# Relation layer of a two-layer graph network: squares on ScalarE and the rows' factor in PSUM, in place of two VectorE operations whose operands both lie in SBUF

## The reference, cut to what matters

```
h_tan   = log_map_zero(h)                                  # per node
msg_tan = einsum('ei,eio->eo', h_tan[src], rel_weight[etype]) + rel_emb[etype]
msg     = tanh(sc*|msg_tan|) * msg_tan / (sc*|msg_tan|)     # sc = 0.1
w       = en / (norm_sum[dst] + 1e-6)
lam     = 2 / (1 - 0.01*sum(msg*msg) + 1e-6)
numer   = segment_sum(w*lam * msg, dst);  denom = segment_sum(w*lam, dst)
h_agg   = project_to_ball(numer / denom)                    # then combined with the loop term
```

## Time and profile before

| | us |
|---|---|
| median of 3 runs | 6124.92 |
| the profiled execution's own time | 6125.32 |
| its span, first to last instruction | 6123.5 |
| POOL busy | 4091.2 |
| VectorE busy | 3449.4 |
| TensorE matmul busy | 2752.4 |
| ScalarE busy | 1127.1 |

### The profile page before, as it was taken

How to read it: one execution, slowest core, us unless ns; L and a number is a source line. 1 busy time by engine, 2 the same in 40 slices (tenths; PEclk the granted TensorE clock), 3 DMA queues, 4 the chain that set the end, 5 groups by cost and what they waited for, 6 DMA issues and landing times.

```text
span 6123.5 us, 55029 instructions
## 1 busy us (share of the span) xinstructions
PE 2752.4 (45%) x13577; PEld 1954.7 (32%) x13578; DVE 3449.4 (56%) x3558; ACT 1127.1 (18%) x1409; POOL 4091.2 (67%) x3714
## 2 busy tenths in 40 slices
PE   2540000000000000000677788788878787877777
PEld 1110000000000000000555566555656565655555
DVE  8601121212122222231688888888888888888887
ACT  3540000000000000000222222222222222222322
POOL 2327777777777777756466666667666666677663
PEclk6555555555555555555788888888888888888888
DMA  5881111111111111101000010001001010101110
GB/s 148 276 252 31 23 28 34 26 36 38 24 39 39 27 35 39 31 5 22 21 21 15 19 29 21 21 21 28 22 21 29 21 29 21 29 21 29 29 29 19
DMA packets 150773, 252.22 MB, mean 41 GB/s; under 512 B 73462, under 2 KB 130315, under 8 KB 135158
## 3 DMA queue, kind: packets, MB, share of 16 engines
q0 software_dynamic: 126224, 100.13, 8.4%
q1 hardware_dynamic: 24431, 151.31, 7.2%
q10 hardware_dynamic: 32, 0.01, 0.0%
HBM read 113.60 MB, written 136.63 MB: 41 GB/s over the span
## 4 chain that ended last, share of the span: by engine, by line
POOL 28%; PE 20%; DVEq 15%; issue 15%; DVE 13%; DMA 6%; POOLq 1%; ACT 1%; SPq 0%; ACTq 0%
POOL arena L354 25%; PE psS L573 9%; DVEq L1226 7%; PE psS L578 6%; DVE stage L1187 4%; DMA table<-arena 4%; PE psW L567 3%; DVE stage L1229 2%; POOL gath L359 2%; DVEq L1194 2%; DVEq L1154 2%; DVE arena L1187 1%; DVEq L1187 1%; DVE work L776 1%; DVEq L1141 1%
## 5 line engine op out<-in xcount | busy, mean ns | idle before, releaser
L359 POOL DMA_INDIRECT gath<-h_dram,hidx x1695 | 1984.1, 1171 | 979.5 <-issue 524.1
L354 POOL DMA_INDIRECT arena<-table,arena x1646 | 1685.1, 1024 | 504.8 <-issue 503.9
L561 PE MATMUL psT<-identb,stage 128*100 128x128 bf16 x2448 | 230.7, 255 | 2382.6 <-DVEq L1141 2366.3
L578 PE MATMUL psS<-stage,ident 128*128 128x256 f32 x3390 | 950.1, 437 | 152.9 <-DVE stage L1229 151.9
L561 PEld LDWEIGHTS psT<-identb,stage 128*100 128x100 bf16 x2448 | 207.7, 153 | 2419.6 <-DVEq L1141 2324.1
L776 DVE TENSOR_TENSOR work<-arena 128x1536 f32<-128x1536 f32 x25 | 44.0, 1759 | 1595.3 <-DMA arena<-table,arena 1595.3
L573 PE MATMUL psS<-arena,ident 128*128 128x256 f32 x3390 | 828.8, 382 | 0.2 <-issue 0.2
L578 PEld LDWEIGHTS psS<-stage,ident 128*128 128x128 f32 x3390 | 719.6, 220 | 310.2 <-DVE stage L1229 195.0
L1187 DVE TENSOR_TENSOR arena<-psW,gath 128x768 f32 (+1 forms) x565 | 522.6, 952 | 482.4 <-DMA gath<-h_dram,hidx 274.2
L567 PE MATMUL psW<-wst,stage 100*128 100x256 bf16 x3390 | 575.6, 290 | 278.6 <-DVE arena L1187 202.8
L573 PEld LDWEIGHTS psS<-arena,ident 128*128 128x128 f32 x3390 | 605.5, 191 | 70.1 <-issue 0.4
(11 more groups left out here) (223 smaller groups left out, 2259.9 us busy)
## 6 DMA issues: line engine op xcount, KB each, us to landing
table<-arena SPq DMA_DIRECT2D x50, 1610.0 KB
ef<-arena SPq DMA_DIRECT2D x22, 1831.1 KB
gath<-h_dram,hidx POOLq DMA_INDIRECT x1695
arena<-table,arena POOLq DMA_INDIRECT x1646, 2.3
arena<-in_edge_attr SPq DMA_DIRECT2D x22, 585.9 KB
table<-arena SPq DMA_DIRECT2D x50, 186.9 KB
arena<-first_dram POOLq DMA_DIRECT2D x1, 915.5 KB, 12.0
info<-info_dram POOLq DMA_DIRECT2D x2, 432.0 KB, 9.2
```

The lines of the kernel that those rows point to most:

```text
L354: pool.indirect_dma_start(out=row4[:, a, q, s, :], out_offset=None, in_=table_d, in_offset=bass.IndirectOffsetOnAxis(ap=pair4[:, a, q, s:s ...
L359: pool.indirect_dma_start(out=gath[:, q, s, :], out_offset=None, in_=rows, in_offset=bass.IndirectOffsetOnAxis(ap=idx[:, q, s:s + 1].bitca ...
L561: last = nc.tensor.transpose(psTb[0:KE, t % 2, j, 0:GP], efs[:, 8 * t + j, :], identb[0:GP, 0:GP])
L578: nc.tensor.matmul(psS[0:GP, IO:2 * IO], ident[0:GP, 0:GP], prod[:, c0:c0 + IO], start=False, stop=False)
```

## The change

ScalarE computes the squares of the gathered rows, between two new semaphores: DVE signals `rows_got` when the rows are there, ACT squares them into `sq` and signals `rows_sq`, and DVE waits for that before its sum. ACT's loop over the pairs becomes a loop over two pairs each, since `row4` has two halves. The factor of each row is written to PSUM (`psS`), and the multiplication of the rows reads it there.

```diff
+        factor = psS[0:GP, 0:2 * S].rearrange("p (q s) -> p q s", q=2)
...
-            with act.Fori(0, pairs) as i:
+            def squares_of_pair(i, a):
+                act.wait_ge(m["rows_got"], i + 1)
+                nc.scalar.activation(sq[:, :, :, 0:D], row4[:, a, :, :, :], ACT.Square).then_inc(m["rows_sq"], 1)
                 act.wait_ge(m["n2_ready"], i + 1)
                 nc.scalar.activation(sl[:, 2, :, :], sl[:, 1, :, :], ACT.Sqrt, scale=CURV)
                 nc.scalar.drain()
                 nc.scalar.activation(sl[:, 3, :, :], sl[:, 2, :, :], ACT.Tanh).then_inc(m["th_ready"], 1)
+
+            with act.Fori(0, (pairs + 1) // 2) as t:
+                squares_of_pair(2 * t, 0)
+                with act.If(pairs > 2 * t + 1):
+                    squares_of_pair(2 * t + 1, 1)
...
                 dve.wait_ge(tgath[a], dve.snap(cum[a]) * 16)
-                tt(y, G, G, ALU.mult)
+                dve.sem_inc(m["rows_got"], 1)
+                dve.wait_ge(m["rows_sq"], i + 1)
                 row_sum(sl[:, 0, :, :], y)
...
-                tt(sl[:, 3, :, :], sl[:, 3, :, :], lam, ALU.mult)
-                V.tensor_tensor(y, G, bc(sl[:, 3, :, :], D), ALU.mult)
+                tt(factor, sl[:, 3, :, :], lam, ALU.mult)
+                V.tensor_tensor(y, G, bc(factor, D), ALU.mult)
```

More of the change, by code:

```diff
@@ L200, in build @@
                  "passed tab_ready wraw_in wsplit win_iota loop_n loop_t "
-                 "bst_ready blk_in tg0 tg1 l0_math n2_ready th_ready hnorm hnorm_out h2_ready h2_out "
+                 "bst_ready blk_in rows_got rows_sq tg0 tg1 l0_math n2_ready th_ready hnorm hnorm_out h2_ready h2_out "
                  "scored start_ready src_in0 src_in1 ef_in idx_ready valid_in mold_ready m0_ready "
```

## The result

| | before | after |
|---|---|---|
| median of the runs, us | 6128.32 (4 runs, 6123.57 to 6133.73) | 6088.74 (4 runs, 6078.07 to 6091.37) |
| profiled execution, us | 6125.32 | 6088.93 |
| its span, us | 6123.5 | 6087.1 |
| first index fetch to last table gather, us | 459.19 to 2712.90: 2253.7 | 460.50 to 2676.05: 2215.6 |

The ratio is 0.9932, 95% interval [0.9915, 0.9949]: 31 to 52 us faster. I had forecast 6086, or 38.5 us less. The relation stage alone became 38.2 us shorter. The table stage ended 1.3 us later, and the rest, from the last gather on, took 0.45 us more; neither has an edit in it.

The account below looks back on a forecast made before the run. POOL's issue of indirect gathers was taken to bound the relation stage. -56.8 + 18.5 - 0.2 = -38.5 us from 6125.32 gave 6086.8, less 0.4 for the median: 6086 us, range 6057 to 6097.

Parts of the forecast that it names:

- The bound: Relation stage: it lasts as long as POOL needs to issue its indirect gathers; a shorter DVE chain alone is worth nothing.
- the tally: Relation-stage gather excess: 34.7 us beside squares, 22.1 beside line 1050, 75.2 in feature pieces, sum 132.0.
- The two removed stretches, -56.8: Gathers beside the squares and line 1050's multiplication are no longer stretched: -34.7 - 22.1 = -56.8 us.
- DVE's chain: Square to reduction in each pair: 1.63 us by way of ScalarE instead of 1.83, bounds 1.5 to 1.9.
- What is given back, +18.5: Feature piece: the shifted cast holds a gather, stretch 4.26 per piece against 3.42, 22 x 0.84 = +18.5 us.
- The place: Start of line 1006's cast within a gather: 0.32 us in, 0.1 to 0.6 with the bounds, formerly 0.73.
- Held: Feature piece: the gather in which the cast starts at 0.32 is held until 0.08 us past the cast's end.
- The last pair's chain: End of the relation stage: the last pair's DVE chain lies on the path and becomes 0.2 us shorter.
- Rival (b): Attention stage: a shifted TensorE clock mixture takes back the gain, +41 us at 0.83, result about 6127; 3%.
- One sign of being wrong: Relation stage: POOL waiting on DVE's line 997 for more than 0.9 us would show the forecast wrong.
- (a): Feature piece: the gather in progress is not held, stretch 3.01 per piece, -66 us, 6059 us; 16%.
- (c) to (e): New form still stretches gathers, 6090 to 6100, 5%; POOL waits at `bst_ready`, 6090 to 6095, 2%; nothing changes, 6125, 2%.

Follow-up runs that it names:

- the kernel without any stretch: Changed kernel with ScalarE making the feature piece's bf16 copies and a PSUM copy of the raw values, residual in PSUM: 5990.77 us, ratio 0.9781.
- the repeated execution: The changed kernel run again, nothing altered, beside the two with a later feature piece: 6085.51 us, ratio 0.9932.
- the kernel with 96 zeros: Changed kernel plus a useless DVE sum of 96 zeros per partition before the feature piece: 6067.17 us, ratio 0.9900.

## Why the prediction was right

**The bound.** POOL's gathers set the stage, and the excess of 132 us lay where the tally had put it. This is shown from both ends: the kernel with more work on DVE was faster, and the kernel without any stretch was 132 us shorter in this stage than the one before (2253.7 - 2121.8).

**The two removed stretches, -56.8.** They went altogether. The rows of another stage with the same kinds of operands were a sufficient witness. (Its timeline has some 600 gathers that start beside line 1187, not 91; none of them takes over 0.98 us.) DVE's output to SBUF, a suspect that those rows did not clear for the squares, is ruled out by the squares into PSUM. The probe that the Trainium skill reports, in which such an operation did not stall DMA ("SBUF — State Buffer", section "Who interferes with whom"), does not hold for these gathers: one is stretched in each of 24 pairs before. The same section of the Trainium skill also says that two SBUF inputs contend with GpSimd's reads, and the runs agree with that.

**DVE's chain.** I had put the reduction 1.63 after the point where the square used to start. It starts 1.52 after ScalarE's square, which in pair 6 begins 0.15 before a gather, where DVE's began 0.14 before one. Over all pairs the mean is 0.14 against 0.19, but in the two other kernels where DVE squares it is 0.11 and 0.13. The way through the semaphore to ScalarE thus cost nothing that stands out from this spread, where I had taken 0.1. Square needed no table load of its own: the load ahead of the square root moved behind the square, beside the reduction, and the count of loads per pair stayed two.

**What is given back, +18.5.** The mechanism was right. The place was forecast at 0.32 and is 0.32 in pair 6, but 0.30 to 0.48 over all, 0.37 on average. The cost was forecast at 4.26 per piece and is 4.26, and that this agrees to the last digit is luck: the later place adds 0.05, and POOL resumes 7.64 after the cast where I had put 7.69, which takes 0.05 off. "Held" was my choice between rows that were 0.19 and 0.67 in; the border is at about 0.5. My bounds for the place, 0.1 to 0.6, reached over it. That all 22 casts of the profiled execution fell short of it, the latest at 0.48 where the first one to wait came at 0.54, was in part luck too. In the repeated execution five pairs fell on the other side, each worth 4.3 - 3.41 = 0.9 us, and its stage is 3.4 us shorter. I did not see that the cast could wait as well. The row was there: in the earlier trace rows the casts take 2095 ns on average, in the changed kernel 2057. That wait is also why POOL resumed 7.69 after the cast's start before and 7.64 after, so it went into the price of the new piece as the 0.05 above, some 1 us over 22 pieces. The price of the old piece was read, not worked out, and has no such error.

The prediction leaned there on the Trainium skill ("SBUF — State Buffer", section "SBUF: two separate sides"). That section gives the shared ports to whichever of the two instructions starts first, which would let the gather in progress keep the cast out. The traces have both cases: 60 casts hold a gather that started before them, and 94 wait for one.

**The rest.** The last pair's chain is on the path as forecast: from the last gather to the first write of the second layer's rows it takes 52.8 instead of 53.1 us. The attention stage kept its length within 1 us (3358.2 against 3357.5 from that write to the end). Rival (b), a different mixture of clocks there, did not occur: in windows of 450 to 600 us from 2900 to 5950, the granted clock is 0.83 to 0.87 before and 0.85 to 0.87 after.

**One sign of being wrong was met by the letter.** I had named POOL waiting on DVE's line 997 for more than 0.9 us. It is 1.2 us, but each of these waits is the gap of 0.30 that stands between any two gathers. The sign was badly chosen; it should have been a gap over 0.30.

**Rivals.** (a) held for none of the 22 pairs in the profiled execution, and for 5 in another; with 0.3 us of added work it can be had for all. Its price was wrong: not 3.01 per piece and 6059, but 3.41, which gives the stage -56.8 and 6068. The stage of the kernel with 96 zeros is 56.9 us shorter than that of the kernel before. Its median, 6067.17, agrees less well than it seems, since the kernel before took 6130.16 beside it, not 6125. (c) to (e) did not occur.

## What to carry to other kernels

- Where GpSimd's indirect gathers bound a stage, look at what VectorE runs beside them, even if VectorE is mostly idle. Here each wide operation with two SBUF inputs, or wide cast, under which a gather started cost the bounding engine what was left of the operation, and a cast did so even when it started up to 0.48 us into the gather. One operand in PSUM, or the work on ScalarE, removed that; ScalarE's 1.5 to 3.2 us operations cost nothing here.
- When one such collision is removed, ask where the next one now falls. The collision beside the multiplication had aligned the two engines for the next one. Squares on ScalarE alone had 34 of 38 us, the factor in PSUM alone next to nothing.

## What the runs showed of the hardware that I had not expected

- A gather of 0.94 us and a wide VectorE cast keep each other waiting, by which comes first. A cast that starts up to 0.48 us in holds the gather (2.43 to 2.61 us), one that starts from 0.54 to 0.76 us in waits itself (2.29 down to 2.07 us instead of 2.06). A multiplication with two SBUF inputs that starts 0.45 to 0.86 us in holds nothing (72 gathers, at most 0.97 us).
- A tensor_tensor that reads the same SBUF tile twice counts as one with two SBUF inputs: 2.44 us for the gather beside it, also with its output in PSUM (2.45).
- The table load before a square root did not have to precede the square: ScalarE ran Square right behind Tanh with no load between.
